# Flamingo block on one core: the order of the batch loop rewritten for PE, ACT, DVE and POOL together

## What is computed

```
x = x + tanh(gx[0]) * attention_1(layernorm(x), ctx)   # 16 heads of 64, keys from ctx (masked) and from x itself: 77 + 128
x = x + tanh(gf[0]) * butterfly_ffn(layernorm(x))      # 128 -> 512 -> gelu -> 512 -> 128; butterfly weights folded at run time
x = x + tanh(gx[1]) * attention_2(layernorm(x), ctx)   # 16 heads of 8; only the 32 largest of 77 scores count
x = x + tanh(gf[1]) * experts(layernorm(x))            # sigmoid(x @ Wr + br), the best of 8 experts, 128 -> 512 -> 128
```

## Time and profile before

| what | us |
|---|---|
| median of 3 runs | 811.86 (810.77 to 813.05) |
| the profiled execution | 816.19 |
| its span, first to last instruction | 814.5 |
| busy: PE, DVE, ACT, POOL | 671.9, 563.6, 484.5, 448.6 |
| first copy of kvT, the last of its sixteen | 27.4, 614.8 |
| last batch's logits have their bias | 745.3 |

### The profile page before, as it was taken

How to read it: one execution, slowest core, us unless ns; L and a number is a source line. 1 busy time by engine, 2 the same in 40 slices (tenths; PEclk the granted TensorE clock), 3 DMA queues, 4 the chain that set the end, 5 groups by cost and what they waited for, 6 DMA issues and landing times.

```text
span 814.5 us, 19311 instructions
## 1 busy us (share of the span) xinstructions
PE 671.9 (82%) x4994; PEld 538.8 (66%) x4994; DVE 563.6 (69%) x3753; ACT 484.5 (59%) x1315; POOL 448.6 (55%) x689
## 2 busy tenths in 40 slices
PE   5498977889898989898989898989898968854696
PEld 4466665767676767667676767777767656543696
DVE  3266415778796969786868787878787889994232
ACT  1166558586767777777776776767776744221231
POOL 6445737565665646473737473737465553753144
PEclk9789999999999999999999999999999985555798
DMA  7200199900000000000000000000000000100672
GB/s 192 60 1 1 37 307 314 304 24 1 2 2 1 0 0 0 0 0 0 0 0 0 0 0 0 0 0 0 0 0 2 1 2 1 40 33 33 194 230 78
DMA packets 38535, 37.88 MB, mean 47 GB/s; under 512 B 3633, under 2 KB 34249, under 8 KB 38484
## 3 DMA queue, kind: packets, MB, share of 16 engines
q1 hardware_dynamic: 32986, 27.76, 12.0%
q10 hardware_dynamic: 3994, 6.36, 2.9%
q0 software_dynamic: 1504, 3.17, 1.1%
HBM read 16.28 MB, written 21.45 MB: 46 GB/s over the span
## 4 chain that ended last, share of the span: by engine, by line
PE 33%; ACT 21%; DVE 15%; issue 13%; POOL 11%; SPq 3%; DMA 2%; POOLq 1%; another core or an unknown queue 0%; DVEq 0%; ACTq 0%
DVE sw L1554 5%; ACT L1183 5%; PE bank L714 4%; ACT prob L1183 4%; PE bank L802 4%; DVE m L1548 4%; ACT sw L1183 3%; PE score_banks L844 3%; PE bank L900 3%; PE bank L1155 3%; POOL second_keys L496 3%; PE bank L814 3%; PE bank L1165 3%; PE bank L868 2%; PE bank L824 2%
## 5 line engine op out<-in xcount | busy, mean ns | idle before, releaser
L1554 DVE MATCH_REPLACE8 sw<-m,sw 128x77 f32<-128x77 f32 x1024 | 220.2, 222 | 0.0
L1548 DVE MAX8 m<-sw 128x8 f32<-128x77 f32 x1024 | 189.3, 226 | 8.7 <-DVE sw L1554 5.1
L1183 ACT ACTIVATE prob<-score_banks,negmax 128x205 f32<-128x205 f32 x256 | 108.2, 433 | 50.2 <-DVE negmax L1496 50.1
L503 POOL TENSOR_TENSOR sw<-sw,m 128x616 f32<-128x616 f32 x64 | 78.0, 1218 | 95.2 <-DVEq L1530 95.1
L484 POOL TENSOR_TENSOR prob<-prob,inv 128x820 f32<-128x820 f32 x64 | 99.4, 1554 | 50.6 <-DVE inv L1501 50.6
L1496 DVE TENSOR_REDUCE negmax<-score_banks 128x2 f32<-128x410 f32 x128 | 68.5, 577 | 62.1 <-PE score_banks L844 62.1
L937 PEld LDWEIGHTS bank<-v,p1T 77*128 77x128 f32 x512 | 73.8, 217 | 34.6 <-issue 20.6
L937 PE MATMUL bank<-v,p1T 77*128 (+1 forms) x512 | 74.5, 273 | 17.2 <-DVE rows_out L1508 12.6
L1554 DVE MATCH_VALUE_LOAD sw<-m,sw 128x8 f32 x1024 | 77.9, 76 | 0.0
L714 PEld LDWEIGHTS bank<-ident,prob 128*77 128x77 f32 (+1 forms) x512 | 57.5, 147 | 19.2 <-issue 18.8
L868 PE MATMUL bank<-ptc,z_ring 77*64 77x128 f32 x512 | 53.5, 284 | 20.0 <-ACT z_ring L1183 18.4
(11 more groups left out here) (234 smaller groups left out, 1508.1 us busy)
## 6 DMA issues: line engine op xcount, KB each, us to landing
z_sorted<-no_row SPq DMA_DIRECT2D x1, 17415.0 KB, 62.9
raw<-in_L_ffn_W ACTq DMA_DIRECT2D x23, 256.0 KB
z_ring<-z_sorted SPq DMA_DIRECT2D x23, 129.0 KB, 3.5
w<-in_L_ffn_W SPq DMA_DIRECT2D x8, 256.0 KB, 4.2
raw<-in_L_xattn_Wkv SPq DMA_DIRECT2D x2, 512.0 KB, 10.8
xs<-in_x SPq DMA_DIRECT2D x1, 960.0 KB, 6.9
cx<-in_ctx SPq DMA_DIRECT2D x1, 577.5 KB
raw<-in_L_xattn_Wq SPq DMA_DIRECT2D x1, 512.0 KB, 10.6
```

The source lines that it names most:

```text
L503: g.tensor_tensor(v, v, m8[:, 4 * q:4 * q + 4, 0, 0:1].to_broadcast([128, 4, 2 * NK]), ALU.subtract).then_inc(s["sub_done"], 1)
L1183: return nc.scalar.activation(dst, src, f, **kw)
L1548: v.max(m8[:, h, r, :], sw[:, h, src, :]).then_inc(s[name], 1)
L1554: v.match_replace(sw[:, h, 1, :], m8[:, h, r, :], sw[:, h, src, :], TAKEN)\
```

## The change

1. **One new list for each of the four engines** (below). The same operations on the same data stand in another order.
2. **P is projected a step earlier**: `keys_T`, the first `keys_in` and the first `queries_in` of a batch move from the start of A's step to slots 6 and 7 of P's step. POOL's `stage_inputs` moves from slot 4 to slot 1, `stage_mask` from slot 7 to slot 6.
3. **Three banks**: besides `GZ` and `OA`, projections may use `TL`: `keys_in` 2 and `queries_in` 1 do. `probs_T` then waits for TL's last reader. `down` and `project_out` move to `GZ`.
4. **Selections in halves**: `top_32` becomes `top_first` (two rounds) and `top_second` (two rounds), with other work between. Pairs 0 to 5 now stand in B's step, pairs 6 and 7 in C's.
5. **The bias at the end**: ACT copies each batch's logits out (`keep_logits`); DVE adds the bias to all batches of a route at once (`route_biases`, three times) before ACT's `route_exps`.
6. The residual after `down` moves to the last place of DVE's list, one step number earlier (for A2), and PE's hardware loop starts at step 7, the others' still at 6.

The core of the diff:

```diff
-        def run_steps(eng, step):
+        def run_steps(eng, step, first=LAGS):
...
+            apart(pool)
             g.tensor_copy(mask_now[:, :], batch(mask_rows, b)).then_inc(s["p_step"], 1)
...
-            def probs_T(b, q):
+            def probs_T(b, q, lag):
                 reach(pe, "p_norm", b, q + 1)
-                reach(pe, "pt_ready", b, q)
+                free("TC")
+                if reader.get("TL") != reader.get("TC"):
+                    free("TL")
...
+                for name in ("TC", "TL"):
+                    read_next(name, "pt_ready", lag, q + 1)
...
-                    last = mm(M[:, 0:D], f_h[:, n, :], w_dn[:, n, :], start=(n == 0), stop=(n == HC - 1))
+                    last = mm(dst[:, 0:D], f_h[:, n, :], w_dn[:, n, :], start=(n == 0), stop=(n == HC - 1))
...
+                        if P is not None:
+                            if i == 1:
+                                pe.wait_ge(s["upb_step"], 6)
+                            keys_T(P, 0)
...
-            run_steps(pe, step)
+            run_steps(pe, step, LAGS + 1)
...
+            def keep_logits(b):
+                reach(act, "lg_psum", b, 1)
+                copy(route[:, bass.ds(b, 1), :].squeeze(1), M[:, 0:NE]).then_inc(s["lg_ready"], 1)
...
             def route_exps(n):
                 b0, b1 = ROUTES[n]
-                act.wait_ge(s["lg_ready"], b1)
+                act.wait_ge(s["r_biased"], n + 1)
...
+            def top_first(b, k):
+                if b is None:
+                    close_top()
+                    return
+                if k % 2 == 0:
+                    reach(dve, "sc_ready", b, k // 2 + 1)
+                apart(dve)
+                top_rounds(b, k, range(ROUNDS // 2))
+
+            def top_second(b, k):
+                if b is None:
+                    return
+                top_rounds(b, k, range(ROUNDS // 2, ROUNDS))
+                open_top[0] = "topk_odd" if k % 2 else "topk_even"
...
+            def route_biases(n):
+                b0, b1 = ROUTES[n]
+                if n == 0:
+                    dve.wait_ge(s["ld_router"], 32)
+                dve.wait_ge(s["lg_ready"], b1)
+                r = route[:, b0:b1, :]
+                v.tensor_tensor(r, r, br[:, :].unsqueeze(1).to_broadcast([128, b1 - b0, NE]), ALU.add)\
+                    .then_inc(s["r_biased"], 1)
...
+                    if (i, slot) in ((17, 0), (20, 0)):
+                        route_biases(0 if i == 17 else 1)
...
+                        if A2 is not None:
+                            reach(dve, "y_psum", A2, 1)
+                            reach(dve, "xb_added", A2, 1)
+                            residual(A2, batch(xs, A2), GZ[:, 0:D], 2, "x2_ready")
```

More of the change, by code:

```diff
@@ L633, in step @@
                         if C is not None:
-                            keep_top(C, 0)
+                            below_max(C, 2)
                         if B is not None:
@@ new lines, in step @@
+                        if E is not None:
+                            context_T(E, 5)
+                        if A is not None:
+                            queries_in(A, "TL", 1, 1, 6)
+                    if slot == 3:
+                        if E is not None:
+                            second_out(E, 5)
+                        if A is not None:
+                            values_in(A, "OA", "lat", 0, 1, 7)
+                            keys_in(A, "GZ", 3, 1, 8)
+                            probs_T(A, 0, 1)
+                        if C is not None:
+                            contexts(C, 1, 4)
@@ L1090, in step @@
-                    if slot == 5:
-                        if A is not None:
-                            values_in(A, "GZ", "ctx", 1, 7)
-                            probs_T(A, 1)
+                            second_scores(B, 1, 3)
                         if A2 is not None:
@@ L1111, in step @@
                                 pe.wait_ge(s["dn_done"], NST)
-                            hidden(A2)
+                            hidden(A2, 2)
+                        if P is not None:
+                            queries_in(P, "OA", 0, 0, 2)
                         if A is not None:
-                            scores(A, 3, 9)
-                        if C is not None:
-                            contexts(C, 2)
+                            attend(A, "GZ", 2, 1, 10)
                         if E is not None:
@@ L1665, in step @@
[L1665 to L1676 removed]
+                    if slot == 0:
+                        if B is not None:
+                            statistics(B, batch(xs, B), b_st, b_mv, "x2_ready", "b_stats")
+                        if E is not None:
+                            context_out(E)
+                        top_first(C, 6)
@@ new lines, in step @@
+                    if slot == 1:
+                        if A is not None:
+                            maxima(A, 0)
+                            maxima(A, 1)
+                        if B is not None:
+                            normal(B, batch(xs, B), b_z, b_mv, b_rs, "brs_ready", "bz_ready")
+                        top_second(C, 6)
+                        top_first(C, 7)
+                    if slot == 2:
+                        if A2 is not None:
+                            reach(dve, "o_psum", A2, 1)
+                            residual(A2, batch(xs, A2), GZ[:, 0:D], 0, "x1_ready")
+                            statistics(A2, batch(xs, A2), f_st, f_mv, "x1_ready", "f_stats")
+                        top_second(C, 7)
+                        close_top()
+                        if A is not None:
+                            inverses(A, 0)
+                            maxima(A, 2)
+                            maxima(A, 3)
@@ new lines, in step @@
+                    if slot == 3:
+                        if A2 is not None:
+                            normal(A2, batch(xs, A2), f_z, f_mv, f_rs, "frs_ready", "fz_ready")
+                        top_first(B, 0)
+                        if E is not None:
+                            reach(dve, "o1_psum", E, 1)
+                            reach(dve, "xo_added", E, 1)
+                            residual(E, last_x(E), M[:, 0:D], 1, "x3_ready")
+                        top_second(B, 0)
+                        top_first(B, 1)
@@ L1677, in between @@
+                    if slot == 4:
+                        if E is not None:
+                            statistics(E, last_x(E), c_st, c_mv, "x3_ready", "c_stats")
+                        if A is not None:
+                            inverses(A, 1)
+                            maxima(A, 4)
+                            maxima(A, 5)
+                        top_second(B, 1)
+                        top_first(B, 2)
+                    if slot == 5:
+                        if E is not None:
                             reach(dve, "rz_kept", E, 0)
```

471 lines of the change are left out of this document (218 added, 253 removed).

## The result

The changed kernel takes **733.75 us** (median of 4 runs, 730.59 to 734.37) against 812.45 (4 runs beside it, 810.77 to 814.45): ratio 0.902 (0.899 to 0.906). The direction was forecast, the size was not: 757 was predicted, with a lowest end of 737. The gain is 79 us where 55 were expected.

What follows compares the result with a forecast made beforehand. PE was taken as nearest bound; a loop step was 34.2 + 0.8 + 1.0 = 36.0 us against 39.7. With the loop's -37.0, all parts summed to -54.7, so 811.9 - 54.7 = 757 us, range 737 to 787.

Steps and rivals of the forecast that it cites:

- the seam's chain: PE waits of 0.62, 0.77, 0.78 and 0.50 us where two steps meet, around kvT; their 2.7 us would go.
- the score ring: Score block, maxima, exponentials and hand-overs before banks are overwritten, 3.4 to 3.6 us; the 1.22 us wait would mostly go.
- so PE's 34.2 stays as the floor: Full step: no matmul goes or comes, so PE's busy time of 34.2 us remains the least step.
- I take 0.8 us: Wait on PE at router_T, before the last score block, for DVE's normal(E): 0.8 us a step.
- in between I take 1.0: Allowance a step for tied score rings: 1.0 us, between 0 (all won) and 1.8 (all waits outside the seam stay).
- step 1: First to second kvT copy, 43.3 us: only the mask is staged sooner, -1.2 us, bounds +2 and -4.
- the drain: Last kvT copy to last logits with bias: step 16, fewer selections, later end of DVE's step and tail, -9.4 us.
- I take four steps of 35.0: Steps 2 to 5, before the loop: 35.0 us each instead of 36.8, together -7.1 us.
- More waits than allowed: Rival, chance 0.22: both tied score rings and router_T lose, step 38 us, total 777.
- the clock falling elsewhere: Rival, chance 0.10: clock falls at other places than the seam, step 37.1 us, total 774.
- DVE late to every score block: Rival, chance 0.06: score rings wait for DVE's half selections, step 41.6 us, total 840, slower than before.
- waits only moved: Rival, chance 0.04: as much idle time as before, total 811 us.

Runs made afterwards that it cites:

- bare variant: Changed kernel with transposes, first keys and queries projections and first score block back at the head of the batch's own step, nothing between: 774.64 us, ratio 0.953.
- less work on DVE: Three instead of four rounds in each selection, 24 of 77 scores kept: 706.09 us in the changed kernel, 803.17 in the kernel before.
- Moving one link of the chain: Kernel before with DVE's add of the router bias half a selection earlier, from slot 7 into slot 6: 816.48 us, ratio 1.003.
- covered early products: Taken away: changed kernel with keys_T and first projections back in the batch's own step, second_probs_T and down before the products: 747.45 us, ratio 0.918.
- last variant: Changed kernel with router_T behind the last score block, ACT and POOL swaps, and POOL's second normalise before add_rows: 724.37 us, ratio 0.888.

## Why the prediction was right in direction and short in size

**The loop (-37.0 predicted, -57.1 measured).** The mechanism was right as far as it went: the seam's chain vanished, the score ring no longer holds PE up, the clock stays at full. The step is 34.00 and not 36.0: all three terms of the sum 34.2 + 0.8 + 1.0 were too large:

- *"so PE's 34.2 stays as the floor"* is the step that failed first and most. PE was busy 33.33 in the changed kernel and 33.06 where nothing interrupts it. So PE's busy time from a trace in which it idles 4.5 us overstated the work by 0.9 to 1.1. That is 9 us in the loop. The bare variant, the new order with 2.7 us of idle, is back at 34.28, so the gaps have a part in it; the order of the matmuls differs too, and the runs show the size, not how it comes about.
- *"I take 0.8 us"* for `router_T`: measured 0.17, another 0.6 a step. The list was counted rightly (its order is the crossing of the ring), but on PE the wait before `second_scores` takes up part of it first; with that wait gone it was 0.27.
- *"in between I take 1.0"* for ties: measured 0.50, all in one place. The middle of the bounds, 0 and 1.8, was no better founded than either end; the upper one assumed that waits outside the seam stay, though the new order moves those too.

34.2 - 33.3 = 0.9, 0.8 - 0.2 = 0.6 and 1.0 - 0.5 = 0.5 make up the 2.0 a step, 20 us. The form of the sum was wrong as well, and only the experiments show it: waits on PE's list were added to PE's work as if each stood alone, and DVE was taken to be "there in time". The period is set by the circle of both; the forecast named its crossing, `router_T`, and nothing of the circle.

Against the profiled execution the forecast missed by 27: 20 here, and 7 in the parts before and after the loop together (14 in steps 2 to 5, 1 in step 1, and 8 the other way in the drain, by the kvT marks). Against the medians it is 23, since the profiled execution of before ran 4.3 above its median and that of after only 0.6.

**Steps 2 to 5 (-7.1 predicted, -21.0 measured).** *"I take four steps of 35.0"* failed. With fewer letters in the step PE has less to do (27.45 in 101.20 to 128.65, and the window is 27.45 long), and the step follows PE. The price for latency of butterfly stages and attention was a guess over a row that showed otherwise: busy 29.4 in the earlier trace rows. The bound given, 34.2 a step, was the busy time of a full step and so no bound here at all. But the miss of 14 is not all real: by the mark of the first `r_z` the whole stretch before it gained 13.9, not 23.3, and the 9.4 between them are the earlier place of kvT's copy in the step.

**Step 1 (-1.2, -2.3)** came out within its bounds; its clock is still 0.79.

**The drain (-9.4, -1.9).** By the kvT mark this error has the other sign. From the last kvT to the last `below_max` it was 117.1 and is 111.6: -5.5, where step 16, fewer selections and the later end of DVE's step were to give -10.7. The gap of 5.2 is smaller than the shift of the mark: kvT's copy now comes earlier in its step, which lengthens this row by the 9.4 by which it shortens those above it. From the eleventh `r_z` to the last logits the gain is 11.3. So by kvT marks alone this row says little about what the drain gained. The tail after that was to cost 1.3 and costs 3.6:

```profile
646.01 1.21 POOL L504 TENSOR_TENSOR sw<-sw,m 128x616 f32<-128x616 f32 x1
...
648.87 0.29 POOL L517 COPY rows_out<-r_z 128x128 f32<-128x128 f32 x1 [0.63 <-DVE r_z L1536]
649.12 0.72 POOL L511 TENSOR_TENSOR p<-sw 128x308 f32<-128x308 f32 x1
```

```profile
650.17 1.88 PE L945 MATMUL bank<-v,p1T 77*128 77x9 f32 x8 [0.63 <-ACT r_zT L1189]
651.90 0.58 PE L972 MATMUL bank<-wr,r_zT 128*128 128x8 f32 x2
652.33 1.11 PE L716 MATMUL bank<-ident,p 128*77 128x128 f32 x4
```

The last `below_max` is at 646.0, the last bias at 663.0: 17.0 against 13.4 in the earlier trace rows (731.89 to 745.28), where 14.7 was priced. `keep_top` (L511) stands behind `keep_input` (L517), as forecast, and that copy waits for `r_z` of batch 14. Not forecast: on PE the last transposes (652.33) stand behind contexts and logits of batch 14. PE runs at half clock there (0.50), but it did so in the kernel before as well (0.50 from 700.0 to 745.3), so the clock doesn't explain the difference. No run moved either item alone, so how the 3.6 divide between them is not shown.

**Steps that held.** `keys_T` far ahead of its use hides ACT's copy. PE has no wait at the third bank. In the steady steps nothing in GZ waits for DVE's residual. The bias is worth nothing. DVE's step is near PE's, and its list is part of the circle; it idles 2.4 a step, where 3 to 5 were forecast. The experts stayed (+0.4).

**The rule of the shared read interface.** The prediction set against itself a page of the Trainium skill, "VectorE: DVE Perf Modes", section "Two Vector instructions with no wait between them", by which DVE's second SBUF read interface is shared with GpSimd (POOL here). The rows agree with it where they can. In the changed kernel all three normalisations have POOL's work beside them for part of their time (groups by shape in three steps; busy, mean ns, idle before):

```profile
L1536 DVE TENSOR_SCALAR b_z<-xs,b_mv,b_rs 128x128 f32 x3 | 2.7, 912 | 0.0
L1536 DVE TENSOR_SCALAR f_z<-xs,f_mv,f_rs 128x128 f32 x3 | 2.4, 796 | 0.0
L1536 DVE TENSOR_SCALAR r_z<-rows_out,c_mv,c_rs 128x128 f32 x3 | 1.5, 484 | 0.0
```

`f_z` took 346 before and takes 796, `r_z` took 874 and takes 484. An order of work decides how long the same instruction is. DVE's busy time in a step rose from 31.36 to 31.63 in sum, where the prediction had feared 1.05. In the changed kernel with less work on DVE and POOL's lists untouched, `b_z` took 564 ns and `r_z` 862, `f_z` 796 as here. In the kernel before, the two short ones (339 and 346) had no POOL work beside them in the step looked at (344.8 and 356.9), the long one (362.1) had. No run changed POOL's work alone, so that POOL is the cause is argued from what runs beside what, not shown.

**The rivals.** More waits than allowed (38 us a step), the clock falling elsewhere, DVE late to every score block, waits only moved: none came. All four looked for ways in which it could be less good than the sum. None asked what would follow if the sum's own terms were padded, and the low end of the range stood at a step of 34.7.

## What stays open

In the kernel before, the clock falls in two steps of three; in the steady steps of every variant of the changed kernel it does not, even with the bare seam. The 1.6 us that a fall costs, two steps in three, are some 11 us of the 57 in the loop. What sets it off was not found. Moving one link of the chain left the falls as they were, six in ten steps. Less work on DVE left three in ten, with PE idle 4.2 us in a short step instead of 4.5. A version of the kernel before with its seam free but the rest unchanged was not tried. The parts, taken away one at a time, are worth 8 (bank), 13 (halves), 13 to 14 (covered early products; 41 if bare) and 0 (bias). The rest of the 79 us was not divided further.

## What to carry to other kernels

Take the floor of a bound engine from a stretch in which it doesn't idle, or count it down: here its busy time in a trace with gaps was 3% above what the same matmuls took without them. If the period stays the same to the hundredth while single waits are taken away, look in the chain for a circle through two strict queues and move the instruction at which it crosses; moves that are worth nothing before may count afterwards. And in a chain of hand-overs that nothing covers, the time of one link taken away can turn up at the next, as here 0.62 did (0.77 became 1.59); give the whole chain cover, or move it.

## What the runs showed of the hardware that was not expected

- The granted clock held 1.00 through 2.7 us of idle time in every steady step of the bare variant, while the kernel before lost it in two steps of three. Its steps with and without a fall idle alike (40.40 - 35.78 = 4.6 and 38.70 - 34.19 = 4.5), so the idle time of a step, as rows show it, does not tell whether a fall will come.
- The same matmuls of one step count as 34.19, 34.28, 33.33 and 33.06 us of busy time with 4.5, 2.7, 0.7 and 0 us of idle, and as 33.20 with none in the last variant. Busy time is higher where there are gaps, but does not follow their amount.
- The same normalisation of 128x128 on DVE took 0.35 us in one order of the work and 0.80 in the other, its form unchanged; in `b_z` it was 0.34 and 0.91.
